# A gated state-space and mixture-of-experts layer on one core: the residual and the expert biases change places, and the first loads their order

## The chip, the cores and the metric

The kernel runs on one core of a Trainium2 chip. The metric is the device time in microseconds of one execution. TensorE does the matrix products, VectorE the scans, ScalarE activations and copies, GpSimd element-wise products and indirect transfers, and SyncE issues most DMAs.

## The reference, cut to what matters

x is 8 batches x 512 tokens x 128 channels, float32, and xn its layer norm. The layer returns x + s * silu(f). The first factor is a selective state-space block, the second a mixture of experts:

```python
# s: 256 inner channels, 64 states; h = norm(xn) scaled and shifted
x_ssm, z = split(h @ Win);  x_ssm = silu(causal_conv4(x_ssm) + conv_b)
dt = softplus(x_ssm @ dt_w + dt_b);  Bt = x_ssm @ Bp;  Ct = x_ssm @ Cp
state = state * exp(dt * A) + (dt * x_ssm) * Bt        # over the 512 tokens
y = (sum over states of state * Ct) + x_ssm * D
s = xn + (y * silu(z)) @ Wout                          # residual xn
# f: 2 shared experts on all tokens, the best 2 of 8 routed ones, hidden width 512
f = xn + sum_shared(mlp(xn)) + sum_top2(gate_e * mlp_e(xn))   # each mlp_e ends with + b2_e
```

So xn enters twice, once in each factor, and the term b2 enters f as (gates and two ones) times (rows of b2).

## The kernel before, in words

**Phases.** A first phase normalizes x, projects it, computes convolution, dt, B and C for all batches, routes the tokens (each gets two slots in a list sorted by expert) and scatters the normalized tokens into that list with 64 indirect DMAs of GpSimd. The second phase is a loop over 8 batches, each with 8 groups of 8 steps, so 64 groups u = 8 b + g. A step handles one state for all 256 channels and 512 tokens.

**A step.** ScalarE makes two decay tiles (line 893, exp). The driving term dt * x * B comes in two kinds. In the five D steps of a group TensorE broadcasts B into a bank (line 1317) and VectorE multiplies it with u (line 1147, two per step). In the three E steps (1, 4 and 7) ScalarE makes diagonal matrices (line 899) and TensorE fills the banks (line 1331, two halves of 16 matmuls, one for each channel half). VectorE runs two scans (line 1157). GpSimd multiplies the state by the C rows (line 666), and TensorE adds the product to y (line 1345). Each engine's order is written out by hand, and the engines wait for each other by counting semaphores. In step i TensorE first prepares the banks of step i+1 and then does what else is due, so all that stands in its step i delays the banks of step i+2. ScalarE works a group ahead of VectorE.

**Beside the steps.** Each group has one tile of the shared experts (shared_tile, line 1387; GELU on ScalarE, line 837; shared_out, line 1392, which adds into the bank ffn_ps). The first 40 groups (batches 0 to 4) also work on one block of 256 sorted tokens of one routed expert: x_rows are loaded (SyncE, line 416), turned by TensorE (line 1398), copied to x_block by ScalarE (line 821) and taken through the expert's two products (lines 1408 and 1416). In the last 24 groups GpSimd gathers the results of the routed experts instead.

**Head of a batch** (its group 0). TensorE opens y with D * x_ssm in step 3 (open_y, line 1292), which needs the loads of load_open. In step 4 it projects the previous batch's gated y into ffn_ps (project_out, lines 1352 and 1353, the last product adding xn by the identity). ScalarE copies it out in its group 1 (evict_attn, line 831), and SyncE stores it. In step 7 TensorE opens the feed-forward sum of the batch: xn by the identity (line 1298) and b2 by the gates (line 1299), before shared_out and the next shared_tile. VectorE gates the previous batch's y after step 2 (gate_y, line 1129).

**Final sums.** FINAL_OF names seven groups, 43, 46, ... 61, for the results of batches 0 to 6. In step 1 of such a group TensorE loads the stored feed-forward sum into block_ps (begin_final, line 1370) and adds the routed rows (add_rows, line 1361) in steps 1 and 2. ScalarE takes SiLU at the end of its group (line 861). GpSimd multiplies by the stored projection, and in the group behind TensorE turns the product back and adds x (turn_back, lines 1374 and 1376). The last batch adds its rows to ffn_ps in steps 3 and 4 of group 63. SyncE loads the operands one group ahead (load_final, lines 445 to 447).

**The start of the second phase.** GpSimd drains its scatters and then adds 8 to product_ready. Scans, products and the loads of the C rows wait for that count. SyncE's queue stands in one order: the first weights, a wait for all scatters, x_rows of block 0, the C rows (two halves of 1 MB), the last dt and u, the store of the gates (line 486), a wait for that store, and then the loads of the batch. ScalarE too waits for the store of the gates before its first decay, since the buffer x_block lay in the same part of the arena as the gates that are stored.

Quoted once, the order of the special actions in TensorE's steps:

```python
OPEN_AT, PROJECT_AT, REOPEN_AT = 3, 4, 7
SUM_AT = {0: (-2,), 1: (-1,), 2: (0,), 3: (1,), 4: (2,), 5: (3,), 6: (4,), 7: (5,)}
HEAD_SUM_AT = {0: (-2,), 1: (-1,), 3: (0,), 4: (1,), 5: (2,), 6: (3, 4), 7: (5,)}
```

## Time and profile before

| | us |
|---|---|
| median of 3 timed runs | 1883.88 |
| their range | 1883.74 to 1885.82 |
| the profiled execution's own time | 1886.5 |
| its span | 1884.5 |
| TensorE busy | 1600.9 (85%) |
| VectorE busy | 1723.1 (91%) |
| ScalarE busy | 1362.7 (72%) |
| GpSimd busy | 1370.9 (73%) |
| mean granted TensorE clock | 0.944 |

The profiled execution is one of its own, beside the timed ones; its rows are in microseconds from the start of its span. The span is from the first to the last instruction, its own time is what the device reports. A float32 matmul shows as two passes, so x2 in a row of 128x512 is one product. The number in brackets is how long the engine stood idle before the row, and who released it.

### The profile page before, as it was taken

What the parts mean: (1) busy time and instruction counts of PE and PEld (TensorE: products, weight loads), DVE (VectorE), ACT (ScalarE), POOL (GpSimd) and SP (SyncE); (2) the same over time, 40 slices, a digit from 0 to 9 for tenths busy, and PEclk for the clock granted to TensorE, in tenths of its full rate; (3) what the DMA queues carried; (4) which work ended last, traced back from release to release, by engine and by line L of the source; (5) the groups of instructions that cost most, each with busy time, mean ns of one, the idle gap of its engine ahead of it and who ended that gap; (6) DMA issues with size and microseconds to landing.
All of it is one profiled execution on the core that took longest, in us unless ns stands there. A gap on an engine that the chain in (4) does not pass through costs nothing.

```text
span 1884.5 us, 41997 instructions
## 1 busy us (share of the span) xinstructions
PE 1600.9 (85%) x12738; PEld 796.3 (42%) x12738; DVE 1723.1 (91%) x1906; ACT 1362.7 (72%) x2511; POOL 1370.9 (73%) x675
## 2 busy tenths in 40 slices
PE   1777539999999899998999899998889988898887
PEld 1543224444444444444444444443334434343333
DVE  6799449999899989998999999998999899999996
ACT  3477448778687778777788767786787587777871
POOL 5036527777677767776777677777999798888985
PEclk9788769999999999999999999998999998999998
DMA  8335455557555755556555656565555654556442
GB/s 236 140 135 185 153 128 126 128 128 159 132 126 128 152 136 129 127 123 153 129 125 128 163 126 126 124 138 127 119 117 123 159 116 97 121 127 129 127 88 65
DMA packets 202367, 249.57 MB, mean 132 GB/s; under 512 B 26082, under 2 KB 104364, under 8 KB 202092
## 3 DMA queue, kind: packets, MB, share of 16 engines
q1 hardware_dynamic: 198164, 239.78, 54.6%
q0 software_dynamic: 4096, 8.40, 1.4%
q8 instruction: 63, 1.03, 0.2%
q14 instruction: 44, 0.36, 0.1%
HBM read 204.00 MB, written 43.66 MB: 131 GB/s over the span
## 4 chain that ended last, share of the span: by engine, by line
PE 32%; issue 23%; DVE 19%; POOL 12%; DMA 5%; ACT 5%; DVEq 2%; SPq 1%; POOLq 0%; ACTq 0%
PE ps L1331 10%; DVE arena L1157 10%; PE ps L1345 9%; POOL arena L666 9%; DVE ps L1147 7%; DMA x_rms_by_expert<-arena,slots 4%; PE ps L1416 2%; ACT arena L893 2%; PE ps L1317 2%; POOL x_rms_by_expert L633 2%; PE ps L1292 1%; ACT arena L899 1%; PE ps L1408 1%; PE ps L1392 1%; SPq L329 1%
## 5 line engine op out<-in xcount | busy, mean ns | idle before, releaser
L666 POOL TENSOR_TENSOR arena<-arena 128x1024 f32<-128x1024 f32 x512 | 1202.7, 2362 | 357.5 <-DVE arena L1157 334.6
L1157 DVE TENSOR_TENSOR_SCAN arena<-arena,ps 128x512 f32<-128x512 f32 x1024 | 1177.5, 1203 | 92.9 <-PE ps L1331 54.9
L893 ACT ACTIVATE arena<-arena,neg_A 128x512 f32<-128x512 f32 (+1 forms) x1024 | 671.5, 713 | 84.4 <-DVE arena L1157 83.2
L1331 PE MATMUL ps<-arena 128*64 128x128 f32 x6144 | 439.7, 287 | 155.3 <-DVE arena L1157 113.8
L1345 PE MATMUL ps<-arena,ident 64*64 64x512 f32 x4096 | 568.6, 627 | 2.9 <-POOL arena L666 2.8
L1331 PEld LDWEIGHTS ps<-arena 128*64 128x64 f32 x6144 | 344.2, 141 | 473.2 <-DVE arena L1157 272.2
L1147 DVE TENSOR_TENSOR ps<-arena,ps 128x512 f32<-128x512 f32 x640 | 406.2, 681 | 11.9 <-PE ps L1317 8.5
L899 ACT ACTIVATE arena<-ident,b_turned 128x128 f32<-128x128 f32 x768 | 242.8, 388 | 0.0
L1345 PEld LDWEIGHTS ps<-arena,ident 64*64 64x64 f32 x4096 | 109.3, 133 | 161.7 <-issue 161.7
L633 POOL DMA_INDIRECT x_rms_by_expert<-arena,slots x64 | 69.5, 1086 | 131.4 <-DVE slots L1109 89.6
L1317 PE MATMUL ps<-b_parts,pick 120*128 120x512 bf16 x320 | 123.5, 386 | 14.0 <-DVE arena L1157 13.5
L845 ACT ACTIVATE arena<-ps,arena 128x256 f32<-128x256 f32 x160 | 67.0, 470 | 82.6 <-PE ps L1408 82.6
L893 ACT ACT_TABLE_LOAD x64 | 82.1, 1283 | 54.9 <-DMA gate_scratch<-arena 32.3
L1416 PEld LDWEIGHTS ps<-arena 128*128 128x128 f32 x640 | 77.4, 191 | 39.3 <-issue 39.3
L1416 PE MATMUL ps<-arena 128*128 128x128 f32 x640 | 92.7, 288 | 0.0
L1408 PE MATMUL ps<-arena 128*128 128x256 f32 x320 | 90.5, 405 | 0.0
L837 ACT ACT_TABLE_LOAD x64 | 82.1, 1283 | 11.2 <-PE ps L1387 10.1
L1387 PE MATMUL ps<-x_rms,arena 128*128 128x512 f32 x128 | 72.1, 646 | 0.7 <-issue 0.7
L1408 PEld LDWEIGHTS ps<-arena 128*128 128x128 f32 x320 | 54.2, 189 | 43.5 <-issue 38.5
L1392 PE MATMUL ps<-arena 128*128 128x512 f32 x128 | 69.3, 623 | 2.5 <-ACT arena L837 2.4
L821 ACT COPY arena<-ps 128x256 f32<-128x256 f32 x40 | 14.8, 371 | 77.8 <-PE ps L1398 77.8
L648 POOL DMA_INDIRECT arena<-routed_by_expert,slots x64 | 63.2, 987 | 9.7 <-issue 6.1
(166 smaller groups left out, 973.2 us busy)
## 6 DMA issues: line engine op xcount, KB each, us to landing
arena<-c_scratch SPq DMA_DIRECT2D x128, 1024.0 KB, 8.7
arena<-w_routed_scaled SPq DMA_DIRECT2D x40, 256.0 KB
arena<-in_L_ffn_W_r_dram SPq DMA_DIRECT2D x40, 256.0 KB
arena<-w_shared_tiles SPq DMA_DIRECT2D x128, 64.0 KB
x_rms_by_expert<-arena SPq DMA_DIRECT2D x1, 5120.0 KB, 23.0
arena<-x_rms_by_expert SPq DMA_DIRECT2D x40, 128.0 KB, 7.2
routed_by_expert<-arena SPq DMA_DIRECT2D x40, 128.0 KB, 8.3
sz_scratch<-arena SPq DMA_DIRECT2D x8, 512.0 KB
```

What stands on the lines that cost most here:

```text
L633: nc.gpsimd.indirect_dma_start(x_sorted_d, bass.IndirectOffsetOnAxis(slots[:, k, j:j + 1], 0), rms_tok[:, j, :], None).then_inc(s[f"x_sort ...
L666: nc.gpsimd.tensor_tensor(products[:, i % RING, :, :], states[:, i % 2, :, :], c_rows[:, i // CG, i % CG, :].unsqueeze(1).broadcast_to((P, ...
L893: nc.scalar.activation(decay[:, 2 * i + h, :], dflat[:, ds(slot + h * L, L)], ACT.Exp, scale=aflat[:, ds(col, 1)]).then_inc(s["decay_ready ...
L899: ins = nc.scalar.activation(b_diag[:, e, c, :], ident[:], ACT.Copy, scale=bt_flat[:, ds(at + c, 1)])
L1147: vector.tensor_tensor(ps[bank][:], uflat[:, ds(slot + h * L, L)], ps[new][:], ALU.mult).then_inc(s["u_b_multiplied"], 1)
L1157: vector.tensor_tensor_scan(states[:, i % 2, h, :], decay[:, m, :], ps[bank][:], 0.0, ALU.mult, ALU.add).then_inc(s["scanned"], 1)
L1317: mm(ps[bank][:], pflat[:, ds(sel, P)], bflat[:, ds(col, L)], start=True, stop=True).then_inc(s["b_broadcast"], 1)
L1331: ins = mm(bank[HP * r:HP * r + HP, c * P:(c + 1) * P], u_turned[:, odd, c, h * P + HP * r:h * P + HP * r + HP], b_diag[:, e, c, :], start ...
L1345: ins = mm(y_ps[r][HP * h:HP * h + HP, :], ident[q, q], products[q, slot, h, :], start=False, stop=False, skip_group_check=True)
L1392: mm(ffn_ps[:], w2_shared, hidden, start=False, stop=last_group).then_inc(s["w2_used"], 1)
L1408: mm(bank[:, (RA, RB)[t % 2]], w1_block[:, t, :], x_block, start=True, stop=True, skip_group_check=True).then_inc(s["tile_made"], 1)
L1416: ins = mm(block_ps[:, k * C:(k + 1) * C], hidden_block[:, t, k * P:(k + 1) * P], w2_block[:, t, :], start=(t == 0), stop=(t == HT - 1), s ...
```

## The change

- The gates' load leaves load_open (N_OPEN 3 to 2). It moves to load_final, which also loads xn of that batch (xn_final), so a final load is five DMAs (N_FINAL) instead of three. For the last batch the gates are loaded during group 62.
- open_ffn is gone: in the head, shared_out itself starts ffn_ps. The two products, xn by the identity and b2 by the gates, are now add_xn_b2, called in begin_final (step 1 of the seven groups) and in step 2 of group 63.
- project_out no longer adds xn, but for the last batch. ScalarE's evict_attn is replaced by VectorE's add_xn, which adds xn while it evicts, after step 6 of the head.
- SyncE issues the first C rows, the last dt and u and the store of the gates before it waits for the scatters and loads x_rows of block 0.
- x_block has a place of its own in the arena (256 columns more), and ScalarE does not wait for the store of the gates.

```diff
         result_out = take(L, "p (j c) -> p j c", c=C)
-        x_block = take(BT)
-        take(P + C)
-        w_spare = take(L)
+        take(BT + P + C)
+        xn_final = take(L)
         assert cur[0] == 6 * TF
...
         b1_block = take(HT)
+        x_block = take(BT)
         w1_shared, w2_shared = take(P), take(C)
...
+            def load_gates(f):
+                sp.dma_start(gates_in[0:E, :], gate_d[:, f * L:(f + 1) * L]
+                             ).then_inc(s["final_loaded" if f < NB - 1 else "last_gates_loaded"], 16)
...
             def load_final(f):
...
                 sp.dma_start(attn_in, attn_d[f]).then_inc(s["final_loaded"], 16)
+                sp.dma_start(xn_final, xn_d[:, f * L:(f + 1) * L]).then_inc(s["final_loaded"], 16)
+                load_gates(f)
...
                     store_result(FINAL_OF[u - 2])
+                if isinstance(u, int) and u == ADD_IN[-1] + 1:
+                    sp.wait_ge(s["final_summed"], NB - 1)
+                    load_gates(NB - 1)
                 load_c(b, g, 1)
...
             load_w2(0, e)
-            for n in range(IN_FLIGHT):
-                sp.wait_ge(s[f"x_sorted{n}"], 16 * TOPK * NT // IN_FLIGHT)
-            load_x_rows(0)
             sp.wait_ge(s["dt_u_made"], NB + 1)
...
             sp.dma_start(gate_d, gates_all).then_inc(s["gates_stored"], 16)
+            for n in range(IN_FLIGHT):
+                sp.wait_ge(s[f"x_sorted{n}"], 16 * TOPK * NT // IN_FLIGHT)
+            load_x_rows(0)
             sp.wait_ge(s["gates_stored"], 16)
...
                                  ).then_inc(s["open_loaded"], 16)
-                sp.dma_start(gates_in[0:E, :], gate_d[:, ds(tb, L)]).then_inc(s["open_loaded"], 16)
...
                 pool.wait_ge(s["silu_ready"], f + 1)
-                pool.wait_ge(s["final_loaded"], 48 * f + 48)
+                pool.wait_ge(s["final_loaded"], 16 * N_FINAL * (f + 1))
                 if f:
...
-            def evict_attn(b):
-                act.wait_ge(s["attn_projected"], b + 2)
-                act.wait_ge(s["attn_stored"], b * 16 + 16)
-                nc.scalar.copy(attn_out, ffn_ps[:]).then_inc(s["attn_evicted"], 1)
...
             def hidden_tiles(u, g, block):
...
-            def group(b, g, slot, head, block, block_before, last=None, project=None):
+            def group(b, g, slot, head, block, block_before, last=None):
                 u = b * E + g
...
                         copy_x_block(u)
-                    if i == 5 and project is not None:
-                        evict_attn(project)
                     if not block and i == 2 and u - 2 in FINAL_OF:
...
                 group(b, 0, slot, True, blocks, not first and (blocks or after_blocks), None if first else b - 1)
-                group(b, 1, slot, False, blocks, blocks, project=None if first else b - 1)
                 if blocks:
-                    with act.Fori(2, E) as g:
+                    with act.Fori(1, E) as g:
                         group(b, g, slot, False, True, True)
                 else:
-                    for g in range(2, E):
+                    for g in range(1, E):
                         group(b, g, slot, False, False, False)
...
             act.wait_ge(s["dt_u_made"], NB + 1)
...
-            act.wait_ge(s["gates_stored"], 16)
             run(0, True)
...
-            def group(b, g, slot, last=None):
+            def add_xn(b, odd):
...
+                dve.wait_ge(s["attn_projected"], b + 2)
+                dve.wait_ge(s["xn_loaded"], b * 16 + 32)
+                dve.wait_ge(s["attn_stored"], b * 16 + 16)
+                vector.tensor_tensor(attn_out, xn_in[:].rearrange("p n t -> p (n t)")[:, ds(odd, L)], ffn_ps[:], ALU.add
+                                    ).then_inc(s["attn_evicted"], 1)
...
+            def group(b, g, slot, last=None, last_xn=None):
                 m0 = (b * E + g) * SCANS
...
                         gate_y(last)
+                    if last is not None and i == 6:
+                        add_xn(last, last_xn)
...
                 slot = b if isinstance(b, int) else dve.snap((b % 2) * (NH * L))
-                group(b, 0, slot, last)
+                group(b, 0, slot, last, None if last is None else dve.snap((last % 2) * L))
                 with dve.Fori(1, E) as g:
...
                 for r in range(2):
-                    mm(y_ps[r][:], diagD[:, r, :], silu_x_in[:, r, :], start=True, stop=True)
...
-            def open_ffn(b, odd):
...
-                pe.wait_ge(s["open_loaded"], b * (16 * N_OPEN) + 16 * N_OPEN)
-                pe.wait_ge(s["xn_loaded"], max(b * 16 + 16, 32))
-                mm(ffn_ps[:], ident[:], xn_in[:, odd, :], start=True, stop=False)
-                mm(ffn_ps[:], b2_sb[:], gates_in[:], start=False, stop=False).then_inc(s["sums_opened"], 1)
+                    ins = mm(y_ps[r][:], diagD[:, r, :], silu_x_in[:, r, :], start=True, stop=True)
+                ins.then_inc(s["sums_opened"], 1)
...
+            def add_xn_b2(bank, xn):
...
+                mm(bank[:], ident[:], xn, start=False, stop=False, skip_group_check=True)
+                mm(bank[:], b2_sb[:], gates_in[:], start=False, stop=False, skip_group_check=True)
...
-            def project_out(b, odd, bank):
+            def project_out(b, bank, with_xn=None):
                 for r in range(2):
                     pe.wait_ge(s["y_gated"], b * 2 + (r + 1))
-                    mm(bank[:], wout_sb[:, r, :], y_gated[:, r, :], start=(r == 0), stop=False)
-                mm(bank[:], ident[:], xn_in[:, odd, :], start=False, stop=True).then_inc(s["attn_projected"], 1)
+                    ins = mm(bank[:], wout_sb[:, r, :], y_gated[:, r, :], start=(r == 0),
+                             stop=(r == 1 and with_xn is None))
+                if with_xn is not None:
+                    ins = mm(bank[:], ident[:], xn_in[:, with_xn, :], start=False, stop=True)
+                ins.then_inc(s["attn_projected"], 1)
...
                     pe.wait_ge(s["result_ready"], f)
-                pe.wait_ge(s["final_loaded"], 48 * f + 48)
+                pe.wait_ge(s["final_loaded"], 16 * N_FINAL * (f + 1))
                 mm(block_ps[:], ident[:], ffn_in, start=True, stop=False, skip_group_check=True)
+                add_xn_b2(block_ps, xn_final)
...
-            def shared_out(u, last_group):
+            def shared_out(u, first_group, last_group):
                 pe.wait_ge(s["w2s_loaded"], u * 16 + 16)
                 pe.wait_ge(s["shared_gelu"], u + 1)
-                mm(ffn_ps[:], w2_shared, hidden, start=False, stop=last_group).then_inc(s["w2_used"], 1)
+                mm(ffn_ps[:], w2_shared, hidden, start=first_group, stop=last_group).then_inc(s["w2_used"], 1)
...
                         pe.wait_ge(s["ffn_evicted"], last + 1)
-                        project_out(last, 1 - odd, ffn_ps)
-                    if head and i == REOPEN_AT:
-                        if last is not None:
-                            pe.wait_ge(s["attn_evicted"], last + 1)
-                        open_ffn(b, odd)
+                        project_out(last, ffn_ps)
+                    if head and i == REOPEN_AT and last is not None:
+                        pe.wait_ge(s["attn_evicted"], last + 1)
                     if i == (REOPEN_AT if head else SHARED_OUT_AT):
-                        shared_out(u, isinstance(g, int) and g == E - 1)
+                        shared_out(u, head, isinstance(g, int) and g == E - 1)
                     if next_t0 is not None and i == NEXT_SHARED_AT:
...
                             turn_back(FINAL_OF[u - 1], block_ps)
+                        if u == NB * E - 1 and i == 2:
+                            pe.wait_ge(s["last_gates_loaded"], 16)
+                            pe.wait_ge(s["xn_loaded"], 16 * NB)
+                            add_xn_b2(ffn_ps, xn_in[:, odd, :])
                         if u == NB * E - 1 and i in (3, 4):
...
-ARENA = 39172
+ARENA = 39428
-N_OPEN = 3
+N_OPEN = 2
+N_FINAL = 5
```

## Rows read from the trace of the kernel before

**Rows 1.** The page's busy shares and a costly group; the groups by form, line 1129.

```profile
PE 1600.9 (85%) x12738; PEld 796.3 (42%) x12738; DVE 1723.1 (91%) x1906; ACT 1362.7 (72%) x2511; POOL 1370.9 (73%) x675
...
L893 ACT ACT_TABLE_LOAD x64 | 82.1, 1283 | 54.9 <-DMA gate_scratch<-arena 32.3
...
L1129 DVE TENSOR_TENSOR arena<-ps,arena 128x512 f32<-128x512 f32 x16 | 10.1, 675 | 4.8 <-issue 4.8
```

**Rows 2.** Timeline, 236 to 276: start, duration, engine, line, [idle before]; landings: C rows, then x_rows.

```profile
236.04 0.94 SPq L396 DMA_DIRECT2D arena<-c_scratch  x2
...
239.36 1.49 SPq L486 DMA_DIRECT2D gate_scratch<-arena  x1
...
254.36 1.47 SPq L499 DMA_DIRECT2D arena<-xs_scratch  x2
...
256.69 2.33 DVE L1157 TENSOR_TENSOR_SCAN arena<-arena,ps 128x512 f32<-128x512 f32 x2 [33.20 <-ACT arena L893]
...
270.17 3.44 PE L1292 MATMUL ps<-arena,diagD 128*128 128x512 f32 x4
...
275.76 1.22 DVE L1157 TENSOR_TENSOR_SCAN arena<-arena,ps 128x512 f32<-128x512 f32 x1 [3.03 <-PE ps L1331]
...
DMA to landing us min/median/max: 9.0/9.0/9.0
...
DMA to landing us min/median/max: 2.2/2.2/2.2
```

**Rows 3.** Timeline, head of batch 0, VectorE.

```profile
293.08 1.22 DVE L1157 TENSOR_TENSOR_SCAN arena<-arena,ps 128x512 f32<-128x512 f32 x1 [2.86 <-PE ps L1331]
```

**Rows 4.** Timeline, head of batch 1, TensorE and VectorE.

```profile
479.07 1.02 PE L1353 MATMUL ps<-xn_in,ident 128*128 128x512 f32 x2
...
480.43 1.29 DVE L1147 TENSOR_TENSOR ps<-arena,ps 128x512 f32<-128x512 f32 x2 [1.38 <-PE ps L1317]
...
486.79 1.12 PE L1298 MATMUL ps<-xn_in,ident 128*128 128x512 f32 x2
...
487.84 1.12 PE L1299 MATMUL ps<-gates_and_ones,b_sb 10*128 10x512 f32 x2
...
491.95 1.22 DVE L1157 TENSOR_TENSOR_SCAN arena<-arena,ps 128x512 f32<-128x512 f32 x1 [2.01 <-PE ps L1331]
...
493.99 1.22 DVE L1157 TENSOR_TENSOR_SCAN arena<-arena,ps 128x512 f32<-128x512 f32 x1 [0.82 <-PE ps L1331]
```

**Rows 5.** Timeline, heads of batches 5 and 7, VectorE.

```profile
1298.21 1.22 DVE L1157 TENSOR_TENSOR_SCAN arena<-arena,ps 128x512 f32<-128x512 f32 x1 [1.75 <-PE ps L1331]
...
1698.90 1.22 DVE L1157 TENSOR_TENSOR_SCAN arena<-arena,ps 128x512 f32<-128x512 f32 x1 [1.66 <-PE ps L1331]
```

**Rows 6.** Timeline, final groups 43 and 61, TensorE and VectorE.

```profile
1350.72 1.02 PE L1370 MATMUL ps<-arena,ident 128*128 128x512 f32 x2
...
1352.47 0.38 PE L1317 MATMUL ps<-b_parts,pick 120*128 120x512 bf16 x1
...
1353.39 1.27 DVE L1147 TENSOR_TENSOR ps<-arena,ps 128x512 f32<-128x512 f32 x2
...
1799.62 0.38 PE L1317 MATMUL ps<-b_parts,pick 120*128 120x512 bf16 x1
...
1801.20 1.27 DVE L1147 TENSOR_TENSOR ps<-arena,ps 128x512 f32<-128x512 f32 x2
```

**Rows 7.** Timeline, the groups behind final groups, 44 and 62.

```profile
1371.67 0.69 ACT L837 ACTIVATE arena<-ps,b1s_sb 128x512 f32<-128x512 f32 x1
...
1373.16 1.13 PE L1392 MATMUL ps<-arena 128*128 128x512 f32 x2
...
1827.92 1.29 DVE L1147 TENSOR_TENSOR ps<-arena,ps 128x512 f32<-128x512 f32 x2 [2.75 <-PE ps L1317]
```

**Rows 8.** Timeline, a stretch of TensorE at the lower clock.

```profile
1386.65 1.98 PE L1331 MATMUL ps<-arena 128*64 128x128 f32 x16 [1.96 <-DVE arena L1157]
...
1392.49 1.22 DVE L1157 TENSOR_TENSOR_SCAN arena<-arena,ps 128x512 f32<-128x512 f32 x1 [1.36 <-PE ps L1331]
```

More of the change, by code:

```diff
@@ L262, in mamba_gated_moe @@
             "attn_projected attn_evicted attn_stored ffn_evicted ffn_stored "
-            "rows_gathered0 rows_gathered1 gate_diag_made final_loaded final_summed silu_ready product_s_g_ready "
+            "rows_gathered0 rows_gathered1 gate_diag_made final_loaded last_gates_loaded final_summed silu_ready product_s_g_ready "
             "result_turned result_ready result_stored c_rows_loaded0 c_rows_loaded1 w1_staged w1_scaled "
@@ L1522, in _ @@
                 ysum(NB * S, i)
-            project_out(NB - 1, (NB - 1) % 2, block_ps)
-            pe.wait_ge(s["final_loaded"], 48 * NB - 32)
+            project_out(NB - 1, block_ps, (NB - 1) % 2)
+            pe.wait_ge(s["final_loaded"], 16 * N_FINAL * (NB - 1) + 16)
             turn_back(NB - 1, hid_ps)
 N_W = 21 + 2
-ARENA = 39172
+ARENA = 39428
 N_MASK = 18
```

## The prediction

> **What bounds the kernel now.** I began with the page's busy shares: VectorE is busy 91% of the span, TensorE 85% [rows 1]. Every scan step of the state costs VectorE two scans and, in five steps of eight, two products before them, and between 300 and 1884 us it is seldom idle. So I looked next for the places where it is idle, in the timeline of VectorE alone, because a change of this size can only act there or by adding work to VectorE. There are three kinds of place.
>
> *The start.* ScalarE sits 32.3 us before its first decay until the store of the gates has landed [rows 1]; VectorE's first scan comes at 256.69 after 33.2 us idle [rows 2]. *The heads of the batches.* TensorE has its most work there, and VectorE waits for it: 1.38, 2.01 and 0.82 us in batch 1 [rows 4]; the same three waits, within 0.04, stand at batches 2 to 4, and in batches 5 to 7, which have no expert blocks, the last two stand alone [rows 5]. *Late groups*, where the final sums add matmuls: there TensorE is just in time [rows 6].
>
> **The change, part by part.** All sums are made against the profiled execution's own time, 1886.5 us (span 1884.5); the three timed runs have a median of 1883.88, 2.6 less, and I carry the difference over at the end.
>
> *Start.* ScalarE no longer waits for the store of the gates, since the block's input no longer lies over them. Its sixteen decays need only what was ready at 222.3. VectorE may scan once GpSimd has drained its scatters, when SyncE issues the first C rows, at 236.04 [rows 2]. Scans 0 and 1 then run at 236; step 2 needs GpSimd's first product, which needs C rows that land 9.0 us after their issue [rows 2], at 245.0; steps 2 and 3 end near 253.6. What is late next? TensorE's step 2 turns x_rows of block 0. Their load is now issued behind the gates' store, at 240.9 instead of 230.6, and must drain behind it: the store is in at 254.36, when SyncE goes on [rows 2], so the rows come at about 255. Then TensorE fills step 4 (2.0 us at the low clock), to 257.9, and opens y, for which the x of batch 0 is loaded, issued at 254.36 to 255.8 as before, one gates' load fewer behind it. I take 259.4 for its landing, between the two landings that the rows show, 2.2 and 9.0 us after issue [rows 2], nearer to the short one because it is 512 KB against 1024. The opening of y stood at 270.17 and the scan after it at 275.76 [rows 2]; all that follows is TensorE's chain. Saved: 270.2 - 259.4 = **10.8 us**. Ends: 12.3 (the fill's end at 257.9 decides) and 5.4 (a landing at 264.8). The order of C rows and of the dt and u stores stays as it is, since they could not go before the drain anyway: nothing for it.
>
> *Head, opening the feed-forward sum.* Two 512-column matmuls go, from 486.79 to the next line at 488.89, so 2.1 us, and they stand in TensorE's chain before the fill for which VectorE waits 2.01 and then 0.82 [rows 4]. *Projection.* The third product of each projection goes, 479.07 to 479.93, 0.86 us, right ahead of the broadcast for which VectorE waits 1.38 [rows 4]. *Residual.* VectorE takes over the eviction, with an addition: nearest row the gating product, same shape with one operand in PSUM, 0.675 us [rows 1]; with the gap 0.71. It is placed before step 7; the projection it waits for is older than step 6's operands, so it waits for nothing, and the store of the previous result is a batch old. Behind it on VectorE stands step 7. Cover is none: it counts in full. The bounds are 0.57, ScalarE's copy of the same bank, and 0.8. ScalarE's saved copy is worth nothing, since in the heads ScalarE waits for TensorE, not the other way round.
>
> - Batch 0 has no projection: its waits were 2.86 [rows 3] and 0.82, and TensorE's 2.1 comes off: **-2.1**.
> - Batches 1 to 4: step 6 begins 0.86 earlier; the addition takes 0.71; a wait of 0.23 in step 7 goes; then the fill of the next group's step 1 is ready at 488.9 and 490.9 by TensorE's own chain, while VectorE, free at 489.7, no longer waits. That step ended at 495.2 and now ends at 492.2: **-3.0 each, -12.0**.
> - Batches 5 to 7: no wait at the broadcast, so only 1.75 + 0.82 - 0.71 = 1.86, at the last 1.77 [rows 5]: **-5.5**.
>
> *Final sums.* The two matmuls go into step 1 of seven late groups, behind the matmul of the loaded sum, at 1350.72. Ahead of them there is nothing to gain, behind them stand the rows' four matmuls and then the broadcast for step 3. Cost of the pair 0.86 + 1.05 to 2.1; I take 2.0. The broadcast is done at 1352.85 and VectorE begins step 3 at 1353.39 [rows 6], so the slack is 0.4 with the signal (0.25 to 0.43 in five of the seven), and the fills that follow are even tighter, with a wait of 0.17 already. So 1.9 shows in these five; in the sixth and seventh the slack is 1.08 at the broadcast [rows 6] and 0.6 at the fill, so 1.4. Sum 5 x 1.9 + 2 x 1.4 = **+12.3**. Ends: 0 and 7 x 2.1 = 14.7. ScalarE's SiLU waits for that sum and comes 2.0 later too; the next group's shared GELU ends at 1372.36 and is wanted at 1373.16 [rows 7], 0.8 of slack, and VectorE's own delay moves the need along. Only after the last of the seven, where VectorE already waits 2.75 behind ScalarE [rows 7], 2.0 - 1.4 = **+0.6** is added. The same pair in the very last group's step 2 falls where TensorE is idle 1.24 us and VectorE has two steps ahead: 0 (if that cover is gone, 0.8).
>
> *DMAs.* SyncE issues two more in seven groups, the gates and 256 KB of xn; they go between 1384 and 1390 in such a group, and the next C rows are due only at 1396: hidden (if not, each would cost its issue, 1.5). Needed more than a group later. The gates' load leaves the opening, where it was last. The last gates' load waits for the seventh sum, some twenty microseconds old by the time it stands in the queue.
>
> Sum: -10.8 - 2.1 - 12.0 - 5.5 + 12.3 + 0.6 = -17.5, hence 1869.0 against 1886.5, and 1866.4 against the median.
>
> **A rule weighed.** In the present trace TensorE falls to half of its clock (1.2 of 2.4 GHz) after idling 1.96 us for VectorE; sixteen fill matmuls then take 1.98 us instead of 1.09, and VectorE waits 1.36 [rows 8]. The Trainium skill, "TensorE: Matmul & The Clock Gate", section "HAM oscillation — how this bites in real kernels", says that an engine left idle between bursts is throttled again and starts each burst cold. By that, a head with less for TensorE to do can turn colder, and part of the gain is given back. The trace agrees that it happens in light stretches. By the rule alone the answer would be the third rival's time.
>
> **Rivals.**
> 1. *The start gives nothing.* Another load that stands behind the C rows, or GpSimd, holds the first group to its old time. For it: the loads share a queue that is busy from 240 to 254. Against: the C rows land at 245, and y is opened 11 us after its data. Time: 1866.4 + 10.8 = 1877.
> 2. *TensorE's late groups absorb the pair.* Fills queued behind are reached early because VectorE starts later, so only half shows. Against: five of seven have a slack under 0.45. Time: 1866.4 - 6.2 = 1860.
> 3. *The clock.* Once in each of the eight heads a stretch at 1.2 GHz, at 1.4 a piece: +11, so 1877.5. Against: the heads' low stretches lie before the opening of y, where nothing is taken away.
> 4. *Slower.* The late final sum holds ScalarE, and with it the shared GELU of the group behind, which holds TensorE, as already seen once with 2.75 us [rows 7]. If each of the seven does this, they cost 2.0 + 2.75 = 4.75, together 33, against 30.4 saved: 1883.9 + 2.9 = 1887. It decides from 4.3 a group on, which needs the slack of 0.8 [rows 7] to vanish wholly, and more.
> 5. *It doesn't do what it says*: the wait for the gates' store goes, but the first decay is held by another landing of the same age. Same time as the first rival; counted there.
>
> **How the numbers follow.** Forecast 0.73, rivals in order 0.10, 0.07, 0.07, 0.03. The forecast's own range is 1860 to 1873, from the ends of the start (-1.5 to +5.4) and of the final sums. To hold eight in ten with rivals 1 and 3 mostly inside, I give 1858 to 1877. No change, within 0.2% (3.8 us, about what a measurement of this kernel can tell), would need two rivals at once: 0.03. Slower 0.03, faster 0.94.
>
> **What would show it.** The first scan at about 236 instead of 256.69, and the scan behind the opening of y near 265. In the heads the waits of 1.38 down to 0.5, and 2.01 with 0.82 gone or nearly; one VectorE addition of 0.68 in each of seven heads. In seven late groups a new wait of about 1.6 at the broadcast of step 3, with some 0.3 to 0.4 behind it. The forecast is wrong if the first scans run early and the opening of y still stands near 270, or if the late groups show no new wait.

## The result, and the profile after

The changed kernel takes 1853.8 us (four runs, 1848.7 to 1858.4) against 1884.2 us (four runs of the kernel before beside it, 1883.7 to 1885.8). The ratio is 0.984, with a 95% interval of 0.981 to 0.987. The forecast was 1866.4, with a range from 1858: the gain of 30.4 us is larger than the range allowed. The profiled execution of the changed kernel took 1851.05 us, so against the profiled one of before (1886.5) it is 35.4 us shorter, and its span is 35.2 us shorter. The comparisons of traces below are between these two; some 5 us of their difference are the choice of the execution, since the medians differ by 30.4. All times below are medians of the fast runs; one run of the kernel with group 1 written out again (5015 us) and one of that with group 7 written out (2234 us) were slow and are left out.

The page after, in its head, busy shares and the row of its DMA queue q14, which loads instructions (packets, MB, share), and then the q14 row of the page before:

```profile
span 1849.3 us, 42108 instructions
...
PE 1592.9 (86%) x12724; PEld 791.8 (43%) x12724; DVE 1725.3 (93%) x1913; ACT 1360.5 (74%) x2504; POOL 1371.9 (74%) x675
...
q14 instruction: 27, 0.22, 0.0%
```

```profile
q14 instruction: 44, 0.36, 0.1%
```

VectorE's busy time is 2.2 us more than before [rows 1]; what went is idle time. The q14 row is easily read past. It belongs to the term that the prediction missed.

To see where the time went I took the start of the first scan of every group in both traces; 64 groups, a difference each. Where that difference changes, time is won or lost. Columns: what was forecast, what the difference did.

| stretch | forecast | measured |
|---|---|---|
| first scans, opening of y | -10.8 | -9.6 |
| rest of batch 0's head | -2.1 | -0.5 |
| heads of batches 1 to 4 | 4 x -3.0 | -4.45, -4.94, -3.30, -3.31 |
| ends of batches 1, 2, 3 | 0 | -4.35, -5.20, -4.39 |
| heads of batches 5 to 7 | -5.5 | -3.63, -0.66, -1.71 |
| seven final sums, and behind the last | +12.9 | +10.8 |
| sum | -17.5 | -35.2 |

The last rows can't be told apart cleanly: group 49 is both the group in which batch 6's head ends and a final group, and it is counted with the head; the +10.8 is what is left of the stretch from group 43 on. Heads and final sums together are +4.8, forecast +7.4.

*The start.* VectorE's timeline after (start, duration, engine, line, operation, count, [idle before and its releaser]):

```profile
236.05 4.59 DVE L1163 TENSOR_TENSOR_SCAN arena<-arena,ps 128x512 f32<-128x512 f32 x4 [10.32 <-POOLq L646]
...
247.76 2.33 DVE L1163 TENSOR_TENSOR_SCAN arena<-arena,ps 128x512 f32<-128x512 f32 x2 [5.93 <-POOL arena L674]
...
257.19 1.22 DVE L1163 TENSOR_TENSOR_SCAN arena<-arena,ps 128x512 f32<-128x512 f32 x1 [3.68 <-PE ps L1338]
266.14 1.22 DVE L1163 TENSOR_TENSOR_SCAN arena<-arena,ps 128x512 f32<-128x512 f32 x1 [7.74 <-PE ps L1338]
...
289.91 1.29 DVE L1153 TENSOR_TENSOR ps<-arena,ps 128x512 f32<-128x512 f32 x2 [1.49 <-PE ps L1324]
```

and TensorE's, in the same stretch:

```profile
254.45 0.69 PE L1409 MATMUL ps<-ident,arena 128*128 128x128 f32 x2 [13.14 <-DMA arena<-x_rms_by_expert]
255.07 1.98 PE L1338 MATMUL ps<-arena 128*64 128x128 f32 x16
259.12 3.78 PE L1300 MATMUL ps<-arena,diagD 128*128 128x512 f32 x4 [2.08 <-DMA arena<-xs_scratch]
262.84 1.99 PE L1352 MATMUL ps<-arena,ident 64*64 64x512 f32 x8
```

The first scan stands at 236.05, forecast 236. The x rows are turned at 254.45 and y is opened at 259.12, released by the landing of its own data; forecast 259.4, before 270.17 [rows 2]. So the chain of loads was read rightly. What follows the opening is slower than the forecast took it: from opening to scan it was 5.59 [rows 2], now it is 7.02, with the y sum in 1.99 where 1.09 stood before. TensorE's granted clock is 0.51 on average from 236 to 266, so nearly all of this stretch runs at 1.2 GHz.

*The heads.* VectorE in batch 1's head, after, with the residual addition that took the projection's third product's place:

```profile
467.97 1.30 DVE L1153 TENSOR_TENSOR ps<-arena,ps 128x512 f32<-128x512 f32 x2 [0.49 <-PE ps L1324]
...
471.41 0.66 DVE L1135 TENSOR_TENSOR arena<-xn_in,ps 128x512 f32<-128x512 f32 x1
...
479.43 1.22 DVE L1163 TENSOR_TENSOR_SCAN arena<-arena,ps 128x512 f32<-128x512 f32 x1 [0.58 <-PE ps L1338]
```

Where 1.38 stood, 0.49 stands; where 2.01 and 0.82 stood, a single 0.58 [rows 4]. The addition waits for nothing. Rows, sizes and places are as forecast.

*A final group.* TensorE and VectorE in group 43, and VectorE in the group behind the last of the seven:

```profile
1307.25 1.02 PE L1380 MATMUL ps<-arena,ident 128*128 128x512 f32 x2
1308.11 1.02 PE L1305 MATMUL ps<-arena,ident 128*128 128x512 f32 x2
1309.06 1.12 PE L1306 MATMUL ps<-gates_and_ones,b_sb 10*128 10x512 f32 x2
```

```profile
1311.61 1.29 DVE L1153 TENSOR_TENSOR ps<-arena,ps 128x512 f32<-128x512 f32 x2 [1.60 <-PE ps L1324]
...
1316.71 1.22 DVE L1163 TENSOR_TENSOR_SCAN arena<-arena,ps 128x512 f32<-128x512 f32 x1 [0.46 <-PE ps L1338]
...
1792.71 1.29 DVE L1153 TENSOR_TENSOR ps<-arena,ps 128x512 f32<-128x512 f32 x2 [1.34 <-PE ps L1324]
```

The forecast wanted about 1.6 with 0.3 to 0.4 behind it. The pair of waits stands in all seven (five times 1.60, once 1.54, once 0.95 at the broadcast, each with 0.46). The smaller one is in the second group, 46; the sixth and seventh, for which the prediction had found more slack, show the full 1.60. The last row answers to 2.75 in [rows 7].

*The ends of batches 1, 2 and 3.* The forecast had nothing here. ScalarE's timeline, before, at the end of batch 1, and VectorE's:

```profile
640.09 0.84 ACT L845 ACTIVATE arena<-ps,arena 128x256 f32<-128x256 f32 x2 [1.46 <-PE ps L1408]
648.00 1.28 ACT L893 ACT_TABLE_LOAD   x1 [7.08 <-DVE arena L1157]
...
657.34 1.22 DVE L1157 TENSOR_TENSOR_SCAN arena<-arena,ps 128x512 f32<-128x512 f32 x1 [2.53 <-PE ps L1331]
660.16 1.22 DVE L1157 TENSOR_TENSOR_SCAN arena<-arena,ps 128x512 f32<-128x512 f32 x1 [1.60 <-PE ps L1331]
```

The same place of the changed kernel, ScalarE:

```profile
649.40 0.84 ACT L848 ACTIVATE arena<-ps,arena 128x256 f32<-128x256 f32 x2 [1.46 <-PE ps L1419]
650.26 1.28 ACT L894 ACT_TABLE_LOAD   x1
```

After its last GELU of a batch ScalarE idles 7.08 us before it loads its table for the next batch's decays. The view names a VectorE scan as the releaser, but VectorE worked on without a gap from before 640 to 654.8; only then, with the two waits shown, did it wait for banks that TensorE fills from what ScalarE makes. In the changed kernel the table load follows the GELU at once. The waits of ScalarE, grouped, say how often; before, the row with "3" is this one, and the view of the changed kernel has no such row:

```profile
ACT L893 <- DVE arena L1157: 21.5, 3, 7.3
```

Three waits, at the ends of batches 1, 2 and 3, and at no other. That is where ScalarE's loop over batches 1 to 4 goes back to its beginning. The change removed ScalarE's copy, and with it the reason to write group 1 of a batch out ahead of the loop over groups, so the body of the outer loop became one group shorter. The DMA view shows what moves meanwhile. Of the kernel before, from 630 to 1215 us, a stretch with all three returns, and then from 641 to 648, the first wait:

```profile
q14 instruction: 16, 0.13, 0.1%
...
q14 instruction: 2, 0.02, 0.8%
```

The changed kernel's view of 630 to 1215 has no row for q14: while its loop turns, nothing is loaded over it. The other two waits of the kernel before have one packet each. The next experiments test the loop's form.

### The profile page after: what moved, and what is told of

The parts are those of the page before. It is cut to its first block, busy times and chain, and to the rows that moved or that the text cites. A ratio compares the mean times of both kernels' runs of the same rounds, so it can differ in the third digit from the quotient of the medians.

```text
span 1849.3 us, 42108 instructions
## 1 busy us (share of the span) xinstructions
PE 1592.9 (86%) x12724; PEld 791.8 (43%) x12724; DVE 1725.3 (93%) x1913; ACT 1360.5 (74%) x2504; POOL 1371.9 (74%) x675
## 4 chain that ended last, share of the span: by engine, by line
PE 29%; issue 27%; DVE 18%; POOL 12%; DMA 7%; ACT 4%; DVEq 1%; SPq 1%; POOLq 1%; ACTq 0%
DVE arena L1163 10%; PE ps L1338 10%; POOL arena L674 9%; PE ps L1352 8%; DVE ps L1153 6%; DMA x_rms_by_expert<-arena,slots 4%; PE ps L1427 2%; ACT arena L894 2%; PE ps L1324 2%; DMA arena<-c_scratch 1%; POOL x_rms_by_expert L641 1%; ACT arena L900 1%; SPq L329 1%; POOL pick L598 1%; PE ps L1403 1%
## 5 line engine op out<-in xcount | busy, mean ns | idle before, releaser
L1153 DVE TENSOR_TENSOR ps<-arena,ps 128x512 f32<-128x512 f32 x640 | 406.3, 680 | 18.3 <-PE ps L1324 17.5
L1324 PE MATMUL ps<-b_parts,pick 120*128 120x512 bf16 x320 | 123.7, 387 | 12.8 <-DVE arena L1163 12.3
```

What stands on the lines that cost most here:

```text
L1153: vector.tensor_tensor(ps[bank][:], uflat[:, ds(slot + h * L, L)], ps[new][:], ALU.mult).then_inc(s["u_b_multiplied"], 1)
L1324: mm(ps[bank][:], pflat[:, ds(sel, P)], bflat[:, ds(col, L)], start=True, stop=True).then_inc(s["b_broadcast"], 1)
```

## The experiments

Each experiment ran beside the kernel before on the same chip. Its median was 1883.4 us beside the kernels with group 1 written out again, with the residual and the loop merged, with the start alone and without the pair; 1885.2 beside those with group 7, with groups 1 and 2 and with the two products; and 1883.3 beside the other four. "Packets" is the count in the q14 row.

### The loop's length

**The changed kernel, with ScalarE's group 1 written out again**

```diff
+                group(b, 1, slot, False, blocks, blocks)
                 if blocks:
-                    with act.Fori(1, E) as g:
+                    with act.Fori(2, E) as g:
```

> The changed kernel, with ScalarE's group 1 of each batch written out again ahead of its inner loop, and nothing else. Theory (the loop over batches of ScalarE's program has become short enough that its branch back finds its instructions): the idle time of about 7 us of ScalarE at the start of batches 2, 3 and 4 comes back, VectorE waits 4 to 5 us at the end of batches 1 to 3, instruction packets of ScalarE's queue (44 before, 27 after) rise again, and the time goes up by about 14, to 1868. Rival (the stall went with the copy that ScalarE no longer does, or with TensorE's shorter heads): no change, about 1854, and no idle time at the batch ends.

Measured: 1873.1 us, ratio 0.9947 (0.9928 to 0.9967). The instructions of each engine's work are the same in number as in the changed kernel. The q14 row names no engine; that it is ScalarE's is read from its count, which goes from 27 to 44 when ScalarE's program alone changes. Its page, and the timelines of ScalarE and VectorE at the end of batch 1:

```profile
q14 instruction: 44, 0.36, 0.1%
```

```profile
635.37 1.28 ACT L894 ACT_TABLE_LOAD   x1 [6.76 <-DVE arena L1164]
...
644.41 1.22 DVE L1164 TENSOR_TENSOR_SCAN arena<-arena,ps 128x512 f32<-128x512 f32 x1 [1.91 <-PE ps L1339]
647.49 1.22 DVE L1164 TENSOR_TENSOR_SCAN arena<-arena,ps 128x512 f32<-128x512 f32 x1 [1.87 <-PE ps L1339]
```

The ends of the three batches lose 4.0, 4.1 and 5.6 us against the changed kernel, 13.8 together. Of the remaining 5.8 up to the last scan of the two traces, 2.3 lie in the start, 1.0 in the groups right behind the three ends and 2.5 in batch 5's head. Start and batch 5 also differ between kernels with the same code there, so no run shows that the loop's form costs these.

**The kernel before, with the residual by VectorE** (and the projection without its product with xn), once with ScalarE's loop merged as in the change and once with group 1 left written out. The part that both share, cut to ScalarE and VectorE:

```diff
-                    if i == 5 and project is not None:
-                        evict_attn(project)
...
+                    if last is not None and i == 6:
+                        add_xn(last, last_xn)
```

> The kernel before, with the residual by VectorE alone (projection without xn, VectorE adds it while it evicts), ScalarE's group 1 inside its inner loop as in the change. Start, opening of the feed-forward sum and final sums stay as before. Theory of the loop: the batch ends give back 14, the four first heads 0.9 each by the shorter projection, so about 1884 - 14 - 3.5 = 1866.5. Rival (the batch ends have nothing to do with ScalarE's loop): 1880.

> The kernel before with the residual sum on VectorE alone, as in the run that gave 1869.5 us, but with ScalarE's group 1 of a block still written out ahead of its loop over groups 2 to 7. Theory (the stalls at the end of batches 1, 2 and 3 come with ScalarE's long loop body, not with its copy): the waits of ScalarE at the starts of batches 2 to 4 (7.1 us at its table load) and VectorE's pairs behind them stay, instruction packets stay at 44, and only what the heads give is left: 1880.5 us (1879 to 1883), so that 11 us of the 14 of the other run are the loop's. Rival (the stalls came with ScalarE's copy of the project_out result and go with it): as the other run, 1869.5 us.

Measured: 1869.5 us merged (ratio 0.9925, 0.9909 to 0.9942), 1880.9 us written out (0.9988, 0.9978 to 0.9998). The merged one has 27 packets and no wait of ScalarE at the batch ends, which shrank by 4.35, 5.19 and 4.39 us, within 0.01 the three numbers of the change. The written-out one keeps the waits:

```profile
ACT L886 <- DVE arena L1158: 22.3, 3, 7.7
```

and has 44 packets. So 11.3 us of the step stand in the loop's form, and moving the residual is worth 2.4 us by itself (the two kernels ran in different sets; by their ratios it is 11.9).

**The changed kernel, with group 7 written out behind the loop, or with groups 1 and 2 ahead of it**

```diff
-                    with act.Fori(1, E) as g:
+                    with act.Fori(1, E - 1) as g:
                         group(b, g, slot, False, True, True)
+                    group(b, E - 1, slot, False, True, True)
```

```diff
-                    with act.Fori(1, E) as g:
+                    group(b, 1, slot, False, True, True)
+                    group(b, 2, slot, False, True, True)
+                    with act.Fori(3, E) as g:
```

> The changed kernel with ScalarE's group 7 of each block written out behind its loop over groups 1 to 6, instead of group 1 ahead of it. Theory (it is the length of the outer loop's body that counts, not which group is written out): instruction packets 40 or more instead of 27, ScalarE idle by 6 us or more at the starts of batches 2 to 4, 4 to 5.5 us more at the end of each of batches 1 to 3 or near it, 1868 to 1873 us. Rival (written-out code costs only where it stands right behind the outer loop's first group): no change, 1854 us.

> The changed kernel with ScalarE's groups 1 and 2 of each block written out ahead of a loop over groups 3 to 7: a still longer body. Theory A (one stall for each return of the outer loop, whatever its length beyond what stays loaded): as with one group written out, 1870 to 1875 us. Theory B (the stall grows with the code that must be loaded again): a second stall in each batch, where group 2 or the inner loop is entered, another 3 to 5 us each in batches 1 to 3, 1880 us or more. Rival (the length of the loop has no part in it): 1854 us.

Measured: 1870.3 us (0.9918, 0.9891 to 0.9944) and 1871.5 us (0.9923, 0.9894 to 0.9953). The first has 44 packets, the page of the second says

```profile
q14 instruction: 45, 0.37, 0.1%
```

and the waits of ScalarE, in this order, are

```profile
ACT L894 <- DVE arena L1164: 22.1, 3, 7.7
```

```profile
ACT L894 <- DVE arena L1165: 23.4, 3, 8.0
```

Which group is written out does not matter. The second written-out group adds one packet and 0.3 us to the longest wait, not a second stall: theory A of that run. The three batch ends cost 4.7, 5.3 and 4.7 us with one group, 5.1, 5.9 and 6.0 with two, against the changed kernel. So it is one stall for each return of the outer loop, paid once the body is too long, and only 2 us more in all for the second group. Where between one and two group bodies beside the loop that length lies, no run here says.

### The other terms

**The start alone, on the kernel before** (arena places, the order of the loads, ScalarE's wait; the last is shown)

```diff
-            act.wait_ge(s["gates_stored"], 16)
```

> The kernel before, with the start alone changed (block tile in its own place, ScalarE doesn't wait for the store of the gates, x_rows loaded behind it). My prediction's term is -10.8; by the trace of the changed kernel the scan behind the opening of y came 9.6 earlier, so 1874.5 with the batch ends as before. If the start has something to do with the batch ends, it is 1860.

Measured: 1873.4 us, ratio 0.9942 (0.9926 to 0.9959). The first scan is 21.0 us earlier, the first scan of group 1 is 9.2 us earlier, and the last scan of all 12.0. The ends of the batches keep their waits.

**The order of the first loads, on the changed kernel**

```diff
+            for n in range(IN_FLIGHT):
+                sp.wait_ge(s[f"x_sorted{n}"], 16 * TOPK * NT // IN_FLIGHT)
+            load_x_rows(0)
             sp.wait_ge(s["dt_u_made"], NB + 1)
```

> The changed kernel with the load of the first block's x rows issued ahead of the wait for dt, u and the first C rows, as in the kernel before. Theory (the first y sum is opened by the x rows' turn at 254 us and by the sorted x rows' landing, and the C rows are not late): the first scan moves back by 0 to 3 us and the opening of y forward by no more than 1: 1854 us (1852 to 1857). Rival (the order of these loads made the start's gain): the first scan is late again by 10 us or more and the time 1862 us or more.

Measured: 1856.0 us, ratio 0.9859 (0.9842 to 0.9877). The first scan comes at 234.42, group 1 within 0.1 us of the changed kernel. The intervals of the two ratios, 0.984 and 0.986, overlap, so the order of the loads is worth nothing that these runs can show; the run above has that gain without the rest of the change, so it is ScalarE's freedom from the store of the gates.

**The pair left out.** The results of batches 0 to 6 lack their xn and b2 terms.

```diff
-                add_xn_b2(block_ps, xn_final)
```

> The changed kernel without the two matmuls (xn and b2) in the seven final sums: it leaves these two terms out of the results of batches 0 to 6. Theory (TensorE is just in time there, the pair is exposed): the waits of 1.6 and 0.46 at these groups go and the time falls by 10 to 13, to about 1842. Rival (the late groups absorb the pair, or the waits are TensorE's clock): less than 4 lower, 1850 or more.

Measured: 1840.5 us, ratio 0.9765 (0.9748 to 0.9782). From the first final group to the last scan the difference from the changed kernel falls by 11.1 us, 1.6 a group on average. Each final group itself gets 1.5 to 2.5 shorter, and VectorE's waits at the broadcast are gone; in group 43 two short ones are left:

```profile
1320.73 1.22 DVE L1163 TENSOR_TENSOR_SCAN arena<-arena,ps 128x512 f32<-128x512 f32 x1 [0.24 <-PE ps L1338]
1330.18 1.22 DVE L1163 TENSOR_TENSOR_SCAN arena<-arena,ps 128x512 f32<-128x512 f32 x1 [0.29 <-PE ps L1338]
```

Part of that is given back elsewhere. VectorE waits 1.34 to 1.37 behind a fill at the lower clock, the pattern of [rows 8], at the end of groups 42, 50, 54 and 60; the changed kernel has one such wait in the whole late stretch, in group 62.

**Two products back in each head**

```diff
+                    if head and i == REOPEN_AT:
+                        pe.wait_ge(s["xn_loaded"], max(b * 16 + 16, 32))
+                        mm(ffn_ps[:], ident[:], xn_in[:, odd, :], start=True, stop=False)
+                        mm(ffn_ps[:], ident[:], xn_in[:, odd, :], start=False, stop=True)
```

> The changed kernel with two 512-column products (ident with xn, twice) put back at step 7 of each head, where the opening of the feed-forward sum stood; the shared product behind them starts the bank anew, so their result is thrown away. Theory (TensorE's own chain holds VectorE there, and the opening's leaving was worth 2.0 in each head, 2.1 with the wait ahead): VectorE's waits behind step 7 are back at 1.7 to 2.0 and 0.8 us, each of the eight heads is 1.7 to 2.4 us longer, together 16: 1870 us (1867 to 1873). Rival (the heads' gain came from the projection's third product and from ScalarE's copy that no longer stands among its tiles): under 0.5 a head, 1854 to 1858 us.

Measured: 1866.1 us, ratio 0.9904 (0.9874 to 0.9934), just below the range of the expectation. VectorE in the head of batch 1 of this kernel:

```profile
481.16 1.22 DVE L1163 TENSOR_TENSOR_SCAN arena<-arena,ps 128x512 f32<-128x512 f32 x1 [1.36 <-PE ps L1338]
483.20 1.22 DVE L1163 TENSOR_TENSOR_SCAN arena<-arena,ps 128x512 f32<-128x512 f32 x1 [0.82 <-PE ps L1338]
```

against 0.58 in the changed kernel: 1.60 more by the waits, 1.72 from group to group, nearly all of the 1.82 that the two products hold TensorE:

```profile
476.39 1.13 PE L1485 MATMUL ps<-xn_in,ident 128*128 128x512 f32 x2
477.35 1.02 PE L1486 MATMUL ps<-xn_in,ident 128*128 128x512 f32 x2
478.21 1.02 PE L1403 MATMUL ps<-arena 128*128 128x512 f32 x2
```

In batches 2 to 4 another 1.5 to 1.7 came on top in the first group of the batch. TensorE and VectorE in batch 2's, there:

```profile
655.49 1.22 PE L1338 MATMUL ps<-arena 128*64 128x128 f32 x16 [2.12 <-DVE arena L1163]
656.67 3.49 PE L1300 MATMUL ps<-arena,diagD 128*128 128x512 f32 x4
...
662.25 1.22 DVE L1163 TENSOR_TENSOR_SCAN arena<-arena,ps 128x512 f32<-128x512 f32 x1 [1.09 <-PE ps L1338]
```

TensorE idled 2.12 us; behind that its granted clock is 0.79 from 654 to 658 and 0.78 from 658 to 662, so part of the opening of y runs at half of the full clock (3.49 where the changed kernel takes 1.98), and the scan behind it waits. This stands in step 3 of the head, ahead of the two products of that head, which stand in step 7. The changed kernel idles for the same time at the same place, and its granted clock is 1.00 from 650 to 664:

```profile
651.71 1.09 PE L1338 MATMUL ps<-arena 128*64 128x128 f32 x16 [2.13 <-DVE arena L1163]
```

**The pair a group earlier**

```diff
+                        if u + 1 in FINAL_OF and i == FINAL_AT:       # FINAL_AT = 5
+                            begin_final(FINAL_OF[u + 1])
                         if u in FINAL_OF and i == 1:
-                            begin_final(FINAL_OF[u])
```

> The changed kernel with the opening of the final sums (their b2 and xn products) moved from step 1 of the group that ends the sum to step 5 of the group before it. Theory (the pair costs what VectorE waits, 1.60 and 0.46 us in each of seven groups, because TensorE meets it where it is already late): five sixths of the 11.1 us that leaving the pair out altogether was worth come back, 1845 us (1842 to 1850), and the waits of 1.60 us at the late groups fall below 0.5. Rival (TensorE has no room in step 5 either, since it waits there for GELU's tiles): the same waits stand two scans later, 1853 to 1856 us.

Measured: **1837.9 us**, ratio 0.9764 (0.9747 to 0.978), the fastest kernel here: 45 us below the kernel before, and 14 to 16 below the changed one (by the ratios and by the medians). The last scan is 10.4 us earlier than in the changed kernel, although batch 1's head lost 1.3. The gain comes in steps, one behind each final group: 0.8 at the first, 1.6 to 2.7 at the other six. The waits of 1.60 are gone; single short ones stand in groups 44 and 46, here:

```profile
1352.12 1.22 DVE L1163 TENSOR_TENSOR_SCAN arena<-arena,ps 128x512 f32<-128x512 f32 x1 [0.31 <-PE ps L1338]
...
1400.30 1.22 DVE L1163 TENSOR_TENSOR_SCAN arena<-arena,ps 128x512 f32<-128x512 f32 x1 [0.29 <-PE ps L1338]
```

The expectation fell short by 7 us. This kernel also moves the product of the loaded sum (L1380 in the changed kernel) out of the tight step, which the pair's removal did not; that this is the surplus was not tried apart. Its ratio is the same as that of the kernel without the pair.

**That, with the x rows first and the second half of the first C rows behind the stores**

```diff
+            load_x_rows(0)
             sp.wait_ge(s["dt_u_made"], NB + 1)
             load_c(0, 0, 0)
-            load_c(0, 0, 1)
             store_dt(NB - 1)
             sp.wait_ge(s["gates_copied"], NB)
             sp.dma_start(gate_d, gates_all).then_inc(s["gates_stored"], 16)
+            load_c(0, 0, 1)
```

> The changed kernel with three edits: the pair a group earlier, the first block's x rows loaded first, and the second half of the first C rows issued behind the stores of the gates. Theory: the waits of VectorE in batch 0's first group (5.9, 3.7 and 7.7 us) get shorter by what the opening of y comes earlier, some 5 us, beside the 9 us of the pair: 1840 us (1836 to 1845). Rival (the opening of y is held by what comes behind the x rows, not by the rows): 1845 us, as with the pair alone.

Measured: 1839.4 us, ratio 0.9769 (0.9753 to 0.9786): the rival's side, no gain over the kernel with the pair alone. The first group's stretch is 1 us shorter than in the changed kernel, of the 5 hoped for.

## Why the prediction was wrong

The sign was right and most rows stand where they were put; the size was wrong because a term was missing.

- **The failed step** is the sentence "ScalarE's saved copy is worth nothing, since in the heads ScalarE waits for TensorE, not the other way round". As to the copy no run speaks against it. But the same edit took one of two written-out groups from ScalarE's outer loop, and the prediction costed the instructions and not the code's shape: 13.9 us between the traces in the change, 13.8 back at the same three places when only the shape is undone, 11.3 in medians between the two kernels with the residual alone. Without this term the difference of the traces is 21.3 and that of the medians 16.5, against 17.5 forecast. The term could have been seen beforehand: 21.5 us in 3 waits of ScalarE on an engine that was not late, exactly at the returns of a loop that the diff touches. Of instruction loading the Trainium skill, "Runtime: NRT & Kernel Launch", section "Instruction fetch mechanics", says that a branch taken to a place outside what is loaded makes the engine fetch before it can go on. The traces agree, with 17 more packets of about 8 KB (0.14 MB), 16 of them in the stretch with the returns, and some 7 us of idle time at each of three returns.
- **Start.** The loads and the opening of y came within 0.3 us of the forecast. Of 10.8 us 1.4 were lost behind the opening, nearly all of it to the lower clock: the opening takes 3.78 instead of 3.44 and the y sum 1.99 instead of 1.09. In the rest of that head only 0.5 of the 2.1 came: VectorE waits 1.49 at 289.91 for a broadcast, ahead of which TensorE waited 1.93 for ScalarE's GELU:

```profile
287.58 1.13 PE L1419 MATMUL ps<-arena 128*128 128x256 f32 x4 [1.93 <-ACT arena L840]
```

  ScalarE's hidden tiles were next in line there, and the prediction did not look for what would be.
- **Heads 1 to 4.** Two gave 3.30, forecast 3.0. The other two gave 4.5 and 4.9, because the kernel before has a stretch of TensorE at 1.2 GHz at the opening of y there (2.97 and 3.48 us instead of 1.98) that the changed one does not have. That was luck: no term of the prediction has it, and the kernel without the pair and the one with the pair a group earlier, whose heads are those of the changed kernel, have such a stretch in batch 1 (openings of 2.55 and 2.59, granted clock 0.79 over the 8 us around) and lose 1.3 us there. The third rival priced the clock the other way, and of its eight stretches none came in heads 1 to 4. But that TensorE had more or less to do in a head does not tell whether its clock falls at the opening. What does, stays open; it was not tried.
- **Heads 5 to 7.** The forecast was 1.86, 1.86 and 1.77; only batch 7, with 1.71, is clean. In batch 5 came 3.63: the two waits went as forecast, and VectorE's wait behind the opening of y fell from 1.85 to 0.83, again by the clock (opening 2.50 instead of 3.53). The 0.66 of batch 6 has a final group's waits in it. That the three add to 6.0, near 5.5, says little.
- **Final sums.** The new waits stand as forecast. The groups that hold them, without 49, got longer by 2.1, 1.5, 1.9, 3.5, 2.7 and 2.7 us, more than the 1.9 and 1.4 of the forecast; groups 44, 51 and 62 between them got shorter by 1.5, 1.2 and 1.4. In 44 and 51 that is VectorE's wait of 1.36 and 1.37 behind a fill at 1.2 GHz [rows 8], which the changed kernel lacks there; without the pair four such waits are there. So in these groups more work for TensorE went with fewer low stretches, as the third rival supposes; that the one makes the other was not tried apart. In 62 the term for ScalarE did not come: VectorE waits 1.34, not 2.75 [rows 7]. The +10.8 against +12.9 is the sum of these. "TensorE's late groups absorb the pair" fell, and so did the slower rival: it needed 4.3 a group, and leaving the pair out was worth 1.6 a group.
- **The range** did not even hold the prediction's own ends. With the start's 12.3 and with 0 for the final sums, both named as ends, the sum comes to 1852.6 us, yet the forecast's own range stops at 1860 and the one given at 1858. The measured 1853.8 lies inside those ends, but for another reason: the final sums cost what they were taken for. Runs of the changed kernel also spread by 10 us, and those of the kernel before by 2 in the four beside it, but by 6 to 9 in the longer series of the experiments, so the 3.8 us taken for what can be told from no change was too small.

## What to carry to other kernels

When a diff changes the form of a loop (a group written out or taken in, a call that goes and lets two bodies become one), cost the form by itself: look in the waits of that engine for idle time that recurs once per turn of the outer loop and names an engine that was not late, and look at the instruction queues' packet counts on the page and in the stretch of the wait. Put matmuls that are not urgent into a step where the engine that waits for TensorE is ahead: moving three products by four steps was worth 14 to 16 us here, as much as leaving two of them out (13 to 14). When a stall of many microseconds goes, follow the chain two links further, not one, and say at which clock the next link runs.

## What the runs showed of the hardware

- ScalarE stands for 6.8 to 8.0 us at each return of a loop whose body is too long, and VectorE loses 4.0 to 6.0 of it. With the head's group and the inner loop as the body the stall is nil, and no instruction packet of q14 moves while the loop turns; with one group more it is 6.8 to 7.7, with two more 7.5 to 8.0.
- A stretch of TensorE at 1.2 GHz in a batch's opening costs 1.1 to 1.7 us, and whether it comes is not told by the idle time ahead of it: 2.12 us with, 2.13 without.
- In six kernels with the change's code at the start and in TensorE's first head, the first scan stands between 235.4 and 238.3, and the first two groups take 69.8 to 71.6 us. So much does one profile leave open of the start.
